# One fused layer: first row tiles' statistics shared between VectorE and ScalarE, first input pair handled by halves

## The reference

```
xn = (x - mean(x)) / sqrt(var(x) + 1e-5)
q, k, v = split(xn @ Wqkv + bqkv)            # 512 features each
attn = softmax(q @ k.T / sqrt(512)) @ v @ Wo + bo
scores = (xn @ Wq_w.T) @ keys.T              # 64 experts, the best 16 kept, softmax of these
z = (xn @ A_w.T) gated per expert            # 64 experts x 8
out = x + attn + (z_gated @ B_w.T) * 2
```

## Time and profile before

| | us |
|---|---|
| median of three runs | 2733.27 |
| lowest and highest | 2730.07, 2737.44 |
| the profiled execution | 2741.71 |
| its span, first to last instruction | 2739.8 |
| PE busy | 2657.7 (97%) |
| DVE busy | 1874.3 (68%) |
| ACT busy | 976.3 (36%) |
| mean granted TensorE clock | 0.992 |

### The profile page before, as it was taken

One profiled execution on the slowest core, in us unless ns is written; L12 is line 12 of the kernel. 1 busy time (PEld: TensorE's weight loads), 2 busy tenths in 40 slices (PEclk: granted clock), 3 DMA queues, 4 the chain that ended last, 5 costly groups with the idle time before them and its releaser, 6 DMA issues.

```text
span 2739.8 us, 32530 instructions
## 1 busy us (share of the span) xinstructions
PE 2657.7 (97%) x11728; PEld 2172.4 (79%) x11728; DVE 1874.3 (68%) x2311; ACT 976.3 (36%) x1289; POOL 513.2 (19%) x446
## 2 busy tenths in 40 slices
PE   6998999999999999999999999999899999999998
PEld 4776878878878788788787888888788878888777
DVE  6956976467755677676847476484975847658587
ACT  3562325623365234433335332224232233222311
POOL 1011000000000001111104431322434241232540
PEclk9999999999999999999999999999999999999999
DMA  8589866454464557766877658568477685856866
GB/s 309 203 297 301 278 203 196 152 169 156 164 207 146 178 180 238 237 211 230 296 279 282 254 201 293 212 255 317 182 289 293 230 303 194 294 222 233 301 256 223
DMA packets 256770, 648.29 MB, mean 237 GB/s; under 512 B 26720, under 2 KB 51424, under 8 KB 252384
## 3 DMA queue, kind: packets, MB, share of 16 engines
q1 hardware_dynamic: 200528, 471.02, 50.0%
q0 software_dynamic: 30224, 111.16, 11.1%
q10 hardware_dynamic: 25856, 63.99, 6.6%
HBM read 499.27 MB, written 146.83 MB: 236 GB/s over the span
## 4 chain that ended last, share of the span: by engine, by line
PE 81%; DVE 7%; DMA 5%; issue 4%; ACT 2%; SPq 0%; ACTq 0%; DVEq 0%; POOLq 0%
PE psum L821 36%; PE psum L1955 14%; PE psum L1957 14%; PE psum L1956 14%; PE psum L756 2%; DMA r_lo<-split_scratch 1%; DMA w_raw<-t_scratch 1%; DVE w_lo L882 1%; DMA stat_scratch<-mv 1%; ACT w_hi L542 1%; DVE part_out L2351 1%; DMA w_raw<-W_blocks 1%; DVE part L875 0%; ACT rows L612 0%; PE psum L2041 0%
## 5 line engine op out<-in xcount | busy, mean ns | idle before, releaser
L882 DVE TENSOR_TENSOR w_lo<-w_raw,w_hi 128x1024 fp32r<-128x1024 f32 x216 | 264.2, 1223 | 374.1 <-ACT w_hi L542 373.9
L542 ACT ACTIVATE w_hi<-w_raw 128x1024 fp32r<-128x1024 f32 x216 | 229.0, 1060 | 696.2 <-PE psum L821 602.6
L821 PE MATMUL psum<-w_hi,s_hi 128*128 128x512 f32 x896 | 350.8, 391 | 16.1 <-DVE w_lo L882 15.5
L821 PE MATMUL psum<-s_hi,w_hi 128*128 128x512 f32 x896 | 353.2, 394 | 11.5 <-DVE s_lo L887 6.7
L821 PE MATMUL psum<-s_lo,w_hi 128*128 128x512 f32 x896 | 351.4, 392 | 0.0
L821 PE MATMUL psum<-s_hi,w_lo 128*128 128x512 f32 x896 | 351.1, 392 | 0.0
L821 PE MATMUL psum<-w_hi,s_lo 128*128 128x512 f32 x896 | 349.4, 390 | 0.0
L821 PE MATMUL psum<-w_lo,s_hi 128*128 128x512 f32 x896 | 349.4, 390 | 0.0
L2152 POOL TENSOR_TENSOR run_sum<-run_sum,prob 128x512 f32<-128x512 f32 x98 | 160.6, 1639 | 290.5 <-ACT prob L1794 283.5
L821 PEld LDWEIGHTS psum<-w_hi,s_hi 128*128 128x128 f32 x896 | 168.5, 188 | 56.6 <-DVE w_lo L882 17.5
L821 PEld LDWEIGHTS psum<-s_hi,w_hi 128*128 128x128 f32 x896 | 169.7, 189 | 52.2 <-issue 13.7
(11 more groups left out here) (200 smaller groups left out, 5065.1 us busy)
## 6 DMA issues: line engine op xcount, KB each, us to landing
r_hi<-split_scratch SPq DMA_DIRECT2D x208, 512.0 KB, 3.5
r_lo<-split_scratch SPq DMA_DIRECT2D x208, 512.0 KB, 4.5
w_raw<-t_scratch SPq DMA_DIRECT2D x120, 512.0 KB, 4.2
w_raw<-W_blocks SPq DMA_DIRECT2D x104, 512.0 KB, 4.2
split_scratch<-rows POOLq DMA_DIRECT2D x56, 512.0 KB, 4.5
part_out<-x POOLq DMA_DIRECT2D x28, 1024.0 KB, 12.8
out<-part_out SPq DMA_DIRECT2D x28, 1024.0 KB, 7.5
rows<-x ACTq DMA_DIRECT2D x26, 1024.0 KB, 5.6
```

Source lines behind the costliest of these rows:

```text
L542: nc.scalar.activation(w_hi[:, s % RAW], w_tile(g, idx, s), ACT.Copy).then_inc(s_whi, 1)
L821: mm = pe.matmul(psum[:, bank, :], stationary, moving, start=(k == 0 and n == 0 and not chained), stop=(k == HK - 1 and n == 2), skip_grou ...
L882: nc.vector.tensor_tensor(w_lo[:, s % RAW], w_tile(g, idx, s), w_hi[:, s % RAW].bitcast(F32), ALU.subtract).then_inc(s_wlo, 1)
```

## The change

It is all in the head of the program, and only for the first group.

- Row tile 2 goes from DVE to ACT: DVE takes tiles 0, 1 and 3 (`OWN0`), ACT takes 2 with `moments` (`OWN` is now 2, 4, 6). Counts of semaphores that other places wait on are adapted.
- ACT runs a square root on one column of ones behind its DMA issues. Its table of functions is loaded there, and the later load in front of the real square root goes.
- On DVE the diagonals of tiles 2 and 3, the low part of the router's weights (`wq`) and the two bias differences (`b_diff`) come behind `rstd_start`, that is, while ACT takes the square root. Before, the last three stood between tiles 0 and 1.
- DVE's subtraction of the mean waits for the mean alone (`s_stat0` at 1). Before, it waited for the reciprocal deviation too.
- The first input pair is multiplied, rounded and subtracted in two halves of one slice (128x512) each, under a new semaphore `s_k0`. PE starts item 0 with the first half; the router's matmuls of that item come after the second half.
- Transfers: SP's second weight tile waits for row tile 2 and not for 3. ACT's load of tile 5 comes behind the square root, those of 6 and 7 behind the first weight tile's rounding. POOL's load of `x12` comes after DVE's third tile and not after the second.

The core of the diff:

```
+OWN = [2, 4, 6]
+OWN0 = [0, 1, 3]
...
-        sp.wait_ge(s_row0[HT - 1], 16)
+        sp.wait_ge(s_row0[2], 16)
         load_w(0, 0, 1)
...
+        act.wait_ge(s_ones, 1)
+        nc.scalar.activation(std[:, 0:1], ones[:, 0:1], ACT.Sqrt).then_inc(s_std, 1)
...
-        for j in range(HT):
-            act.wait_ge(s_tiles, j + 1)
-            act.dma_start(own_rows(HT + j), x[(HT + j) * P:(HT + j + 1) * P, :]).then_inc(s_row0[j], 16)
+        act.wait_ge(s_tiles, 1)
+        own_load(HT)
+        moments(0, OWN[0])
         square_roots(1, slice(0, HT))
+        act.wait_ge(s_tiles, 2)
+        own_load(HT + 1)
         for a in range(2):
             act.wait_ge(s_spread, a + 1)
             nc.scalar.activation(mean_rstd[:, a, 0:W], psum[:, 6 + a, :], ACT.Copy).then_inc(s_stat0, 1)
             if a == 0:
                 split_weights(0, 0, 0)
-        split_x(0, 0, 0)
+                own_load(HT + OWN[0])
+                act.wait_ge(s_tiles, 3)
+                own_load(HT + 3)
+        act.wait_ge(s_k0, 1)
+        nc.scalar.activation(s_hi[:, 0, :], xb[:, 0, 0, :], ACT.Copy).then_inc(s_k0, 1)
+        act.wait_ge(s_xn[0], 1)
+        nc.scalar.activation(s_hi[:, 1, :], xb[:, 0, 1, :], ACT.Copy).then_inc(s_shi, 1)
...
-                    if side == 0:
+                    halved = static(g) and (g, idx, s) == (0, 0, 0)
+                    if halved:
+                        pe.wait_ge(s_k0, 3)
+                    elif side == 0:
                         pe.wait_ge(s_slo, pair(g, idx, i) + 1)
...
+                        if halved and a == 1:
+                            pe.wait_ge(s_slo, 1)
...
-        pool.wait_ge(s_tiles, 2)
+        pool.wait_ge(s_tiles, 3)
```

More of the change, by code:

```diff
@@ L282, in phase_a @@
     s_x12 = sem("s_x12")
+    s_k0 = sem("s_k0")
     s_moments = sem("s_moments")
@@ L597, in x_load, with own_load @@
                           .rearrange("(a p) t -> p a t", p=P)).then_inc(s_x[block][p], 16)
+        def own_load(j):
+            act.dma_start(own_rows(j), x[j * P:(j + 1) * P, :]).then_inc(s_row0[j - HT], 16)
         def rows_load(g, j):
@@ L604, in moments @@
             if static(g) and g == 0:
-                tile = own_rows(j)
-                chain = Chain(act, s_moments, (j - HT) // 2 * STAT_STEPS)
-                act.wait_ge(s_row0[j - HT], 32)
+                tile = first_rows(j) if j < HT else own_rows(j)
+                chain = Chain(act, s_moments, OWN.index(j) * STAT_STEPS)
+                act.wait_ge(s_row0[j % HT], 16 * (j // HT + 1))
             else:
                 tile = rows[:, j % 2, :]
-                chain = Chain(act, s_moments, (g * NTOK - NTOK + len(OWN_AT) + j) * STAT_STEPS)
+                chain = Chain(act, s_moments, (g * NTOK - NTOK + len(OWN) + j) * STAT_STEPS)
                 act.wait_ge(s_rows[j % 2], 16 * (g * HT - HT + j // 2 + 1))
@@ L825, in body @@
                                 mm.then_inc((s_kq, s_zv)[side], 1)
-                        if routed and a == 0:
+                        if routed and a == (1 if halved else 0):
                             which, bank, block_k = ROUTED[idx, side]
@@ L973, in normalise_end, with stats_of_tile @@
                                     ).then_inc(s_xn[block], 1)
-        def stats_of_tile(j):
-            chain = Chain(dve, s_stat, (min(j, HT) + max(j - HT - 1, 0) // 2) * TILE_STEPS + (RSTD_STEPS if j > HT else 0))
+        def stats_of_tile(j, n):
+            chain = Chain(dve, s_stat, n * TILE_STEPS + (RSTD_STEPS if j > HT else 0))
             if j < HT:
@@ L990, in stats_of_tile, with mean_diagonal @@
                 return
+            if j < 2:
+                mean_diagonal(j)
+        def mean_diagonal(j):
             if j == 0:
@@ L1099, in vector @@
         nc.vector.memset(wq[:].bitcast(F32), 0.0).then_inc(s_wq, 1)
[L1100 to L1110, removed]
-        rstd_start(slice(0, HT))
-        rstd_finish(1, HT * TILE_STEPS, slice(0, HT))
+        for n, j in enumerate(OWN0):
+            stats_of_tile(j, n)
+        dve.wait_ge(s_mv, HT - 1)
+        dve.wait_ge(s_amv, 1)
+        rstd_start(slice(0, HT))
+        mean_diagonal(2)
+        mean_diagonal(3)
+        dve.wait_ge(s_wq, 2)
+        nc.vector.tensor_tensor(wq[:, :, RD:2 * RD], wq_raw[:], wq[:, :, 0:RD].bitcast(F32),
+                                ALU.subtract).then_inc(s_wq, 1)
+        nc.vector.tensor_tensor(b_diff[:, 0:2], b_col[:, BIAS[0][0]:BIAS[0][0] + 2],
+                                b_col[:, BIAS[1][0]:BIAS[1][0] + 2], ALU.subtract).then_inc(s_bias, 1)
+        nc.vector.tensor_tensor(b_diff[:, 2:4], b_col[:, BIAS[0][2]:BIAS[0][2] + 2],
+                                b_col[:, BIAS[1][2]:BIAS[1][2] + 2], ALU.subtract).then_inc(s_bias, 1)
+        rstd_finish(1, (HT - 1) * TILE_STEPS, slice(0, HT))
         dve.wait_ge(s_rstd, 1)
@@ L1192, in body @@
                         if s == 4:
-                            dve.wait_ge(s_mv, HT + 2)
-                            rstd_ready(len(OWN_AT), slice(HT, NTOK))
+                            dve.wait_ge(s_mv, HT + 1)
+                            rstd_ready(len(OWN), slice(HT, NTOK))
                         if s == 5:
-                            rstd_finish(2, (HT + 2) * TILE_STEPS + RSTD_STEPS, slice(HT, NTOK))
+                            rstd_finish(2, (HT + 1) * TILE_STEPS + RSTD_STEPS, slice(HT, NTOK))
                             dve.wait_ge(s_rstd, 2)
@@ L1281, in load_b11 @@
             if s == 0:
-                pool.wait_ge(s_amv, len(OWN_AT) + NTOK)
+                pool.wait_ge(s_amv, len(OWN) + NTOK)
             tile_free(*((2, PART + s) if s < PART else (3, s - PART)))
@@ L1323, in store_part @@
                            out_split(n).bitcast(F32)).then_inc(s_ust[n % 2], 16)
-        pool.wait_ge(s_amv, len(OWN_AT) + NTOK * (NG - 1))
+        pool.wait_ge(s_amv, len(OWN) + NTOK * (NG - 1))
         for name in ("b21", "b22", "b11", "b12"):
```

26 lines of the change are left out of this document (18 added, 8 removed).

## The result

| | before | after |
|---|---|---|
| median of 18 runs each | 2737.56 | 2728.74 |
| lowest and highest | 2730.07, 2741.83 | 2724.92, 2736.45 |
| span of the profiled execution | 2739.8 | 2726.9 |
| first product | 32.60 | 25.27 |
| third item's first matmul | 47.1 | 40.8 |

The ratio is 0.9971, 95% interval [0.9963, 0.998]: 0.29% faster, 7.9 us at 2737 (the two medians lie 8.8 apart). The forecast was 0.29%. The interval covers both sides of the 0.3% bound. In absolute terms the forecast was 2725.4; the 18 runs of the kernel before lie 4.3 above the three that it started from, and the changed kernel's 3.3 above the forecast.

The account below looks back on a forecast made before the run. PE was taken as the bound, busy 2657.7 of 2739.8 us, idle in the head behind DVE's chain. Starting the first product 3.68 + 0.34 + 3.80 = 7.82 us earlier took 2733.27 to 2725.4 (0.29%), range 2720.0 to 2730.5.

Parts of the forecast that it names:

- Start of the last tile: DVE's statistics of row tile 3 in the head start when it lands, at 14.07, 3.61 us earlier.
- ScalarE's tile 2: ACT finishes row tile 2 at 16.1, 1.0 us ahead of DVE's need at 17.17, so costed at nothing.
- the third rival: ACT's row tile 2 ends late, at 19.1, and DVE waits: 2 us lost, 2727.4; chance 0.04.
- To the reciprocal: On DVE, from epsilon to reciprocal takes 0.94 instead of 1.28, starting at 18.11: 0.34 us won.
- To the spread deviation: From reciprocal to the spread deviation's arrival stays 4.49, hence 22.60; subtraction and weight tile's low part done by 22.2.
- To the first product: From the spread deviation to PE's first product, halves take 2.18 instead of 5.98: 3.80 us won, product at 24.8.
- My 3.18 for tile 2 and 0.48 and 1.60 for the router weights: DVE's earlier costs in the head: tile 2 3.18, wq and biases 0.48 plus 1.60 idleness before them.
- The early table load: ACT's 1.28 us load before the square root is hidden at the start; moved DVE work fills most of that room.
- The slow start: PE's first nine matmuls after the wait start about 0.43 apart, costing 1.8 us, left as it is.
- the rival: The short spreading matmuls count as PE activity and the slow start goes: at most 1.8 us more, 2723.6; chance 0.08.
- The transfer rival: Row tile 4 lands only at 35.8, PE waits 4.5 for item 2, gain 3.3: 2730.0; chance 0.07.
- More slow restarts, and slower than before: Three later PE waits restart at half clock, 3.1 each, losing 9.3: 2734.8, 1.5 slower; chance 0.03.

Follow-up runs that it names:

- the controls: The changed kernel measured again twice with no edit; ratios to the kernel before 0.998 and 0.9975.
- a3: Changed kernel with row tile 2 back on VectorE, ACT taking only tiles 4 and 6; ratio to the kernel before 0.997.
- d2: Changed kernel with the router weights' low part and biases again between row tiles 0 and 1; one run, no ratio, first product at 24.46 us.
- a2: Changed kernel without the early square root on ones, so the table loads before the real square root; ratio to the kernel before 0.9962.
- b2: Changed kernel with 48 unused 128x320 matmuls in PE's pauses of the head; ratio to the kernel before 0.9985.
- c1: Changed kernel with both 48 unused matmuls in the head and the x12 load behind the first pair; ratio to the kernel before 0.9978.
- a4: Changed kernel with SP's second weight tile after row tile 3 and the x12 load after VectorE's second tile again; ratio to the kernel before 0.9967.
- b1: Changed kernel with GpSimd's x12 load behind the first pair's low part; ratio to the kernel before 0.9973.
- c0: Changed kernel again with no edit, as a control; ratio to the kernel before 0.998.
- b3: Changed kernel with row tile 3 loaded as two halves of 1024 columns; ratio to the kernel before 0.9978.

## Why the prediction was right, step by step

- *The place and the mechanism.* PE's first product moved, and the chain from it carried the shift: 7.33 at the first product, 6.3 from the third item to 130 us, 7.6 at 177 us. The forecast of 0.29% was met by the runs. That it was met to the digit is luck: the head gave 7.33 and not 7.82, some of that was lost again by the third item, later restarts gave more back, and the controls measured 0.20% and 0.25%.
- *Start of the last tile:* 14.07 forecast, 14.21 measured, and VectorE waits for the landing there. *ScalarE's tile 2:* 16.1 forecast, 16.15 measured; the third rival's wait is not there.
- *To the reciprocal:* forecast 18.11, measured 18.57. This is the step that was mis-sized. The diagonals cost 0.70 and not 0.38, since the change moved GpSimd's issue of `x12` to 17.05, right beside them. I had written that this load is read much later, which is true, and had not looked at what its issue runs beside. Four kernels with the issue elsewhere had 0.39.
- *To the spread deviation:* 4.49 forecast, 4.48 measured. *To the first product:* 2.18 and 2.22.
- *What each edit is worth.* My sum went along the path and came out well, but it gave each piece of the path to the edit in front of it, and that was wrong. Measured at the first product by taking one edit back: the early subtraction 2.3, the halves 1.5, tile 2 on ScalarE 1.0, the early table 0, the new order of SP and GpSimd -0.3, the router weights' move -0.5 (the last two from tile 3). That makes 4 of 7.3. The other 3 us belong, by the rows, to edits that cover for each other: tile 2 and the router weights both made VectorE late for tile 3, and removing either is enough to come near its landing (VectorE starts tile 3 at 17.68 before, at 15.40 in a3, at 13.88 in d2). No kernel took both back, so this share is worked out and not measured. My 3.18 for tile 2 and 0.48 and 1.60 for the router weights are all real costs before, but not of a single edit.
- *The early table load:* I had said that of its 1.28 most is filled with moved instructions. It needs no early load at all (a2).
- *The slow start:* I left it as it is, at eight. It was 13, 6 and 14 in three profiles of the changed kernel, so it gets shorter or longer and never went as in the rival; the 1 us lost to it at the third item is one of single executions. The sentence from the Trainium skill (TensorE: Matmul & The Clock Gate, Part 1: The HAM clock gate), that sustained activity releases the half-rate clock, is borne out by b2 and c1, where PE's 48 extra matmuls left no slow start. The spreading matmuls alone did not do it.
- *The transfer rival* was closer than I gave it credit for: the third item's weight tile needed 13.0 us and not 10.5, and landed at 35.5. In a4 and b1, with GpSimd's load elsewhere, it needed 10.6 and 11.1, so this is the same oversight as with the diagonals: the change put `x12`'s 2 MB right ahead of it. It cost nothing only because the slow starts delayed PE by as much: the third pair's low part was ready at 38.98, and PE came for it at 40.84 (in c0, with six slow starts, at 39.38). In b2 it cost 2.49.
- *More slow restarts, and slower than before:* not so for the changed kernel. Its mean granted clock was 0.993 to 0.994 over all executions of its three measurements, and the kernel before had 0.993 in the calls of the controls. It did fall in the two kernels with PE kept busy, to 0.991 on average (0.989 to 0.993 over 22 executions).

Left open: why the head's last 3 us in c1 are gone by the end. Slow restarts are part of it, 1.6 us at 562 us in the one profile, and the lower mean clock over its 12 executions (0.991 against the control's 0.993) fits that. What sets their timing was not tested.

## What to carry to other kernels

Follow the engine that is waited for up to the landing of its last input, and ask for each edit what comes late if it is the only one made: two edits that remove the same lateness are worth one. When a transfer is moved, look at what runs beside its issue, not only at when its data is read. And measure a gain at the head again a few items later, since the next late transfer or the next busy engine takes it back.

## What the runs showed of the hardware

- Two of VectorE's 128x128 diagonals beside a software-queued load's issue on GpSimd (1.03 us for 2 MB) took 0.70 together, and 0.39 elsewhere. Elsewhere each of the two takes 0.28. Beside the issue they took 0.71 and 0.58, and both ended only behind its end at 18.08 (18.11 and 18.18). In ns:

```profile
L1018 DVE TENSOR_SCALAR score<-ident,mv x2: 584/648/712, 17.4 to 17.6; 128x128 f32<-128x128 f32 x2
```

  They had started 0.35 and 0.55 after the issue's start. Not everything beside an issue is slowed. In the kernel before the issue began at 14.16, and both the diagonal at 14.31 (0.28) and the `bn_stats` from 14.50 (2.47 for four) kept their times:

```profile
14.16 1.03 POOL L1295 DMA_DIRECT2D xb<-xT  x1 [12.47 <-DVEq L986]
```

  Whether the two were slowed or held until the issue ended, these runs do not settle, since in all kernels with 0.70 the issue starts at the same distance from them.

- Matmuls of 128x512 that start 0.43 apart, which is what 512 columns take at the 1.2 GHz level, stand in a stretch whose granted clock the profile gives as 1.00 (changed kernel, busy times from 25 to 31 us):

```profile
25.00:31.00 6.00, 5.73 (x14) 4.50 (x15) 5.97 (x7) 3.79 (x5) 0.00 (x0) 1.00 1.02 404
```

  Fourteen matmuls fit into it. In b2, 28 did in the same stretch. At the head the distance of starts has to be read, not the column.
- Splitting one 1 MB load into two made the second half land 1.4 us later than the whole had, and the engine's next issue took 2.34 us in place of 0.35 (b3).
